# Unread products of ones on TensorE in the sort of a mixture-of-columns stage

## The reference, cut to what matters

```python
logits = similarity + gate_values                 # 3584 tokens x 16 columns
_, top_idx = jax.lax.top_k(logits, 1)             # each token takes one column
weights = mask * jax.nn.softmax(logits, axis=-1)
cols = gelu(einsum('bsd,cdn->bscn', x, W_cols) + b_cols) * weights[..., None]
y = cols.reshape(B, S, -1) @ proj_w + proj_b + x
out = (y - mean(y)) * rsqrt(var(y) + 1e-5) * ln_g + ln_b
```

## Time and profile before

| | |
|---|---|
| median of 3 runs (range) | 1322.56 us (1321.2 to 1325.54) |
| the profiled execution, its time | 1323.45 us |
| its span | 1321.7 us |
| mean granted TensorE clock in it | 0.902 of full speed |
| PE, DVE, ACT, POOL busy over the span | 91%, 73%, 52%, 47% |

### The profile page before, as it was taken

How to read it: one execution, slowest core, us unless ns; L and a number is a source line. 1 busy time by engine, 2 the same in 40 slices (tenths; PEclk the granted TensorE clock), 3 DMA queues, 4 the chain that set the end, 5 groups by cost and what they waited for, 6 DMA issues and landing times. The chain is left out here.

```text
span 1321.7 us, 32068 instructions
## 1 busy us (share of the span) xinstructions
PE 1197.4 (91%) x12219; PEld 858.6 (65%) x12219; DVE 962.6 (73%) x1653; ACT 680.9 (52%) x1515; POOL 616.0 (47%) x872
## 2 busy tenths in 40 slices
PE   4789899999999998699999999999999969289992
PEld 4565678778877875366667676676766647165551
DVE  7777665775576567788888888888888756725665
ACT  5755112112211222577788778888888753225552
POOL 1327888887885001733333333333333109443774
PEclk9999899999999998599999999999999988655555
DMA  8505445454453202966666666666666204232440
GB/s 235 131 2 188 139 138 174 128 148 150 139 159 109 71 1 48 159 107 98 97 97 97 95 96 100 97 96 95 95 95 95 37 2 140 83 98 68 135 128 29
DMA packets 102277, 138.87 MB, mean 105 GB/s; under 512 B 9614, under 2 KB 84857, under 8 KB 99909
## 3 DMA queue, kind: packets, MB, share of 16 engines
q1 hardware_dynamic: 87428, 91.42, 35.5%
q0 software_dynamic: 14720, 45.68, 12.1%
HBM read 107.63 MB, written 31.41 MB: 105 GB/s over the span
## 5 line engine op out<-in xcount | busy, mean ns | idle before, releaser
L1268 DVE TENSOR_REDUCE s_neg_max<-banks 112x3 bf16<-112x1461 f32 (+1 forms) x192 | 290.2, 1511 | 45.9 <-PE banks L1384 45.7
L1182 ACT ACTIVATE s_prob<-banks 128x448 f32<-128x448 f32 x512 | 272.8, 545 | 92.4 <-PE banks L1410 77.4
L713 DVE TENSOR_TENSOR s_m<-banks,s_base 128x512 f32<-128x512 f32 x256 | 161.2, 683 | 100.1 <-PE banks L867 99.9
L1410 PE MATMUL banks<-s_q_t,s_k_t 112*128 112x112 bf16 x2048 | 186.7, 215 | 1.1 <-ACT s_prob L1182 1.0
L1410 PEld LDWEIGHTS banks<-s_q_t,s_k_t 112*128 112x128 bf16 x2048 | 124.4, 98 | 72.9 <-issue 50.6
L867 PE MATMUL banks<-s_gate_sel,s_tw 64*128 64x256 f32 x1024 | 131.9, 397 | 1.9 <-DVE s_m L713 1.7
L910 PE MATMUL banks<-s_m,s_act_t 128*112 128x256 f32 x512 | 128.2, 388 | 1.5
L1426 PE MATMUL banks<-s_prob,s_v 128*32 128x112 f32 (+1 forms) x4096 | 126.1, 263 | 1.1 <-ACT s_prob L1182 0.7
L892 PEld LDWEIGHTS banks<-s_x_t,s_m 128*128 128x128 f32 x1024 | 116.7, 192 | 10.6 <-issue 8.0
L892 PE MATMUL banks<-s_x_t,s_m 128*128 128x112 f32 x1024 | 122.4, 278 | 0.0
L807 ACT ACT_TABLE_LOAD x8 | 10.3, 1283 | 207.1 <-PE banks L892 207.1
(11 more groups left out here) (301 smaller groups left out, 2262.9 us busy)
## 6 DMA issues: line engine op xcount, KB each, us to landing
k_parts<-s_k_split POOLq DMA_DIRECT2D x64, 281.2 KB, 3.6
s_k_t<-k_parts SPq DMA_DIRECT2D x32, 562.5 KB, 8.3
s_tw<-in_tw SPq DMA_DIRECT2D x16, 1024.0 KB, 5.6
s_k_raw<-in_ctx_k POOLq DMA_DIRECT2D x64, 187.5 KB, 3.8
s_k_t<-k_parts SPq DMA_DIRECT2D x32, 375.0 KB, 5.4
s_v_raw<-in_ctx SPq DMA_DIRECT2D x32, 256.0 KB
s_src<-in_ctx SPq DMA_DIRECT2D x8, 896.0 KB, 15.0
s_k_t<-k_parts SPq DMA_DIRECT2D x32, 187.5 KB, 9.2
```

What stands on the lines that cost most here:

```text
L713: nc.vector.tensor_tensor(dst[:, :, :, rows_], got, base[:, :, rows_].unsqueeze(2).broadcast_to([P, 2, B, HR]), ALU.add).then_inc(S["merge ...
L1182: nc.scalar.activation(prob[t % 2][:, c, :], w.bank(SCORE + n % SRING, P, TILE), ACT.Exp, scale=DH ** -0.5).then_inc(S["exp_done"], 1)
L1268: nc.vector.tensor_reduce(neg_max[half][:, ROWS + first:ROWS + end, 0], w.banks[0:T, MAX:MAX + end - first, 0:NKEY], AX.X, ALU.max, negate ...
L1410: last = nc.tensor.matmul(w.bank(SCORE + n % SRING)[:, s * T:(s + 1) * T], k_t[k][0:ROWS_MAX, h, c * P:(c + 1) * P], q_t[k][0:ROWS_MAX, h, :],
```

## The change

Four groups of bf16 matmuls, whose stationary operand is the tile of ones and whose moving operand is `keep` (ones and zeros), are written to bank 7, which nothing reads at that time. There are 24 of 512 columns ahead of the wait for `cum_done` (behind a new wait for `counting`, the tiles that POOL fills with ones and zeros), 36 ahead of the wait for `token_done`, 16 behind the wait for `slots_done`, and one of 256 columns at the end of each round of the loop. As bank 7 is taken by them, the output products rotate over three banks and not four, and output(n) waits for the sum of tile n-3 and not of tile n-4.

```diff
-                    nc.vector.scalar_tensor_tensor(out=y_of(n), in0=w.bank(4 + n % 4, P, D), scalar=weight[:, n:n + 1],
+                    nc.vector.scalar_tensor_tensor(out=y_of(n), in0=w.bank(4 + n % 3, P, D), scalar=weight[:, n:n + 1],
...
+                def busy(count, cols=512):
+
+                    for _ in range(count):
+                        nc.tensor.matmul(w.bank(7, P, cols), ones16[:], keep[:].rearrange("t c b -> t (c b)")[:, 0:cols],
+                                         start=True, stop=True)
+
+                wait(pe, "counting", 2)
+                busy(24)
                 wait(pe, "cum_done", 1)
...
+                busy(36)
                 wait(pe, "token_done", 1)
...
-                    wait(pe, "summed", n - 3)
-                    nc.tensor.matmul(w.bank(4 + n % 4, P, D), hid_c[n % 2][:], proj[:, bass.ds(c * D, D)],
+                    wait(pe, "summed", n - 2)
+                    nc.tensor.matmul(w.bank(4 + n % 3, P, D), hid_c[n % 2][:], proj[:, bass.ds(c * D, D)],
                                      start=True, stop=True).then_inc(S["y_ps"], 1)
 
                 wait(pe, "columns_done", 1)
                 wait(pe, "slots_done", 1)
+                busy(16)
                 turn(0)
...
                     if n >= 1:
                         output(n - 1)
+                    busy(1, 256)
                 output(N_TILES - 1)
```

## The result

The changed kernel takes 1315.22 us (median of 20 runs, 1311.71 to 1323.48), the kernel before 1324.01 in the same series (20 runs, 1319.02 to 1329.17). The ratio is 0.9947, 95% interval 0.9934 to 0.9959: faster by 0.4 to 0.7%, where no change was forecast (1324.7). The profiled execution took 1315.0, close to the median, with a span of 1313.2 against 1321.7.

A forecast was written before the change was run, and what follows sets the result against it. PE was taken to set the loop's pace at the low clock. Table -7.0, entry -0.6 and half products +9.7 summed to +2.1, so 1324.7 us against the median; the forecast's own range 1320 to 1330, over the cases 1304 to 1334.

The forecast's parts named there:

- What bounds: From 1130 us on PE is either waiting or on the chain, and sets the loop's pace at 2.81 us a round.
- The 24: Products in the first wait, 13.7 us for the count: hidden, cost nothing, gain nothing.
- Three banks: Output banks in the loop: DVE's 0.48 us sum is done two rounds earlier, so three banks cost nothing.
- The 36 and the table: Products in the second wait raise the clock after 5 us; the table then takes 6.8 to 7.0 us, gain 7.0.
- The 16 and the entry: Products in the third wait take 3.5 us warm, cost nothing; clock falls at loop entry after two tiles, gain 0.6.
- the gap of 1.2 us: At the loop's entry PE idles 1.2 us after the 16, then does thin work, so the clock falls.
- The half product: One each loop round, costing 0.23 us in the low clock; 42 rounds make +9.7.
- Rival E: In the loop the ones cost a change of shape, 0.44 us a round: +10.9, 1333.5 us; chance 0.12.
- The sum: Whole kernel: -7.0 - 0.6 + 9.7 = +2.1, against the median 1324.7 us.
- Rival B: Clock holds at loop entry and falls at ACT's table loads after tile 9: -8.8, 1313.8 us; chance 0.24.
- Rival A: Clock holds through the loop and POOL's gathers and scatters become late next, ending 1289.9: -32.7; chance 0.13.
- The rule weighed in the prediction: Long idle gaps cost the clock and successive matmuls keep it; by it the loop stays warm and rival A comes.

The follow-up runs named there:

- the kernel with 48: Changed kernel with 48 products in place of 36 ahead of the table, the 16 kept, no 24 and no half products: 1316.17 us, ratio 0.9918.
- the last kernel: 48 products ahead of the table, 24 behind the slots, gathers 18 ahead, four products in each ACT stop, no first-wait 24 or half products: 1289.87 us, ratio 0.9744.
- kernel with gathers 18 ahead: Kernel with only the 16 added products, gathers issued 18 tiles ahead on POOL's queue instead of 5: 1309.43 us, ratio 0.9897.

## Why the prediction was wrong

- *What bounds.* Right: PE set the pace of the loop, and when it ran 1.2 us a round faster, the kernel ended earlier by what that saved.
- *The 24.* Right: hidden, no gain. *Three banks.* Right: 1.0006, interval over 1.
- *The 36 and the table: wrong by the clock's timing.* I took 5 us in the cold; it was 2.2 us, the 36 ended 2.4 us early, and the table had the clock for one us. It got 0.9 us shorter and not 7.0. The price of a warm table was right (6.8 to 7.0 forecast, 7.2 in the kernel with 48).
- *The 16 and the entry: the step that failed.* "I expect the clock to fall here, after two tiles: gain 0.6." It held for 15 tiles, and entry and warm rounds gave 11.9 us. The step rested on the one above: with a cold table the 16 take 5.7 us and not 3.5, and the gap of 1.2 us from which I argued does not exist. Under the condition that I had assumed, a warm table, the kernel with 48 fell at the entry in its profile, and by their times in five more of its eight runs. So the argument on the gap held where there was a gap in most runs, and the error was to carry one guess for the time of the clock's rise through two steps. Where the count of the products has to meet a wait, both cases belong into the sum.
- *The half product.* 0.14 a cold round, not 0.23, which is less than its columns alone (0.21): the transposition behind it shortens by 0.19. I had written that its own change of shape goes, and put no number to it. As only 27 rounds paid it and not 42, it cost 3.8 us and not 9.7. Rival E (0.44) fell.
- *The sum.* Forecast -7.0 - 0.6 + 9.7 = +2.1; measured in the trace -0.5 - 11.9 + 3.8 = -8.6. The table term and the half product erred by 6.5 and by 5.9 in opposite directions and all but cancel; what is left is the entry.
- *Rival B* was the nearest, 1313.8 for 1315.2, and that close by luck: it had a table gain of 7.0 that was not there, 8 warm rounds where there were 14, and 0.23 a cold round. Its mechanism, a clock that holds at the entry and is lost at ACT's stop, is what two of the traces with the gathers 5 ahead show; in the changed kernel's own trace the fall came later, within the wait for row 15, so there either can have taken it. *Rival A*: the last kernel took 1289.9, the number worked out for A. That is chance as well, as it has other edits, a clock that falls at 1243.9, and another order of gathers and scatters.

The rule weighed in the prediction, of the Trainium skill ("TensorE: Matmul & The Clock Gate", section "Why this matters for your kernels"), that it is long idle gaps that cost the clock, holds only in part here: the clock fell at 1158.1 with PE busy, after 2.4 us of idle time, and in the kernel with gathers 18 ahead after idle times of 0.3 and 1.1 us. What the prediction took as the trace's agreement with the same page of the Trainium skill on transposes is none: ahead of the fall at 1093.0 stood 16 products of 16 columns, and at 1089.6 the clock was up right behind 16 transpositions (1085.4 to 1088.7) and 1 us of dense products.

## What to carry to other kernels

Unread products are worth trying where an existing stall ends in a long stretch of PE-bound work, and they should last until that work starts: 16 of them gave 1% here, and the same 16 run warm, ending 0.9 us early, lost the loop's clock in six runs of eight. Count them for either clock that PE may have when they start, as a longer burst at the end of a wait costs less than a gap: 24 lost it in none of four. Inside a loop look for the stalls ahead of a fall of the clock (here a stop of ScalarE, or a late gather) and fill or remove those, all of them, in place of paying in every round. And before you name one stall as the cause, look at the moment of the fall in more than one trace: with the gathers 5 ahead, two traces here put it between the two stalls, two within the second, and one right behind it.

## What the runs showed of the hardware that was not expected

A bf16 product of 256 columns between two float32 products of differing shape costs 0.14 us at 1.2 GHz where its columns take 0.21: 0.33 us of its own less 0.19 that the next instruction pair gets shorter. The same kernel can fall into two groups of times that go with the granted clock: 48 and 16 took 1302.5 and 1302.8 us at a mean of 0.926 to 0.928, or 1316 to 1319 us at 0.911 to 0.913. And the clock can fall while PE is busy: in the kernel without the half products it did so after 2.4 us without idle time, behind a wait of 1.11 us.
